# A Householder tridiagonalisation on one Trainium2 core: pivot and divisor as one VectorE operation, placed ahead of a y completion, and part of the next column's seed moved from GpSimd to VectorE

## The reference, cut to what matters

```python
def _L0_gnn_ref(features, A, W1, b1, W2, b2):
    deg = jnp.sum(A, axis=0) + jnp.sum(A, axis=1) - jnp.diagonal(A)
    d_inv_sqrt = jnp.where(deg > 0, jax.lax.rsqrt(deg), 0.0)
    L = jnp.diag(deg) - A
    L_norm = d_inv_sqrt[:, None] * L * d_inv_sqrt[None, :]
    _, U = jnp.linalg.eigh(L_norm)                 # 256 x 256
    agg = jnp.einsum('mn,bnd->bmd', U.T, features)
    h = jax.nn.relu(agg @ W1 + b1)
    return jnp.einsum('nm,bmd->bnd', U, h @ W2 + b2)

h = jnp.maximum(_layernorm(x), 0.0)                # x: 32 x 256 x 128
x = x + _L0_gnn_ref(h, adj, ...)
h = jnp.maximum(_layernorm(x), 0.0)
x = x + _L1_gnn_ref(h, adj, ...)                   # two graph layers, then LSTM windows of 1 to 4 rows
```

## Time and profile before

| | us |
|---|---|
| median of 3 runs | 1600.31 (1600.16 to 1602.43) |
| the profiled execution | 1604.85 |
| its span | 1603.0 |

### The profile page before, as it was taken

How to read it: one execution, slowest core, us unless ns; L and a number is a source line. 1 busy time by engine, 2 the same in 40 slices (tenths; PEclk the granted TensorE clock), 3 DMA queues, 4 the chain that set the end, 5 groups by cost and what they waited for, 6 DMA issues and landing times.

```text
span 1603.0 us, 25379 instructions
## 1 busy us (share of the span) xinstructions
PE 1272.1 (79%) x6001; PEld 1068.2 (67%) x6001; DVE 1246.9 (78%) x6154; ACT 610.2 (38%) x2116; POOL 397.3 (25%) x2138
## 2 busy tenths in 40 slices
PE   6999999999986667777354554365999999999997
PEld 5788888888875555555233333163778789999997
DVE  7999988888788888888899999996772345556555
ACT  1222222222233434322122222251334677878775
POOL 5333333434345555555200000002000010000000
PEclk9999999999999999999977776687999989999999
DMA  7000000000000000000000000000000000001001
GB/s 171 1 1 1 1 1 1 2 1 1 1 1 1 1 1 1 1 2 1 1 0 1 0 1 1 0 1 0 1 1 1 0 1 1 1 1 27 1 27 54
DMA packets 23404, 12.66 MB, mean 8 GB/s; under 512 B 5075, under 2 KB 22230, under 8 KB 23254
## 3 DMA queue, kind: packets, MB, share of 16 engines
q1 hardware_dynamic: 23254, 11.03, 2.8%
HBM read 6.83 MB, written 4.19 MB: 7 GB/s over the span
## 4 chain that ended last, share of the span: by engine, by line
DVE 46%; PE 37%; issue 8%; POOL 7%; ACT 2%; DVEq 1%; POOLq 0%
PE bank L824 8%; PE bank L826 5%; PE bank L833 4%; PE bank L669 4%; DVE A L1046 4%; DVE RC L1134 4%; DVE O L1142 4%; PE bank L672 3%; DVE pa L1130 3%; DVE O L1138 3%; PE pair L824 3%; DVE junk L993 2%; DVE zc L1040 2%; DVE wk L1030 2%; DVE O L1023 2%
## 5 line engine op out<-in xcount | busy, mean ns | idle before, releaser
L672 PEld LDWEIGHTS bank<-O 128*128 128x128 f32 x764 | 201.5, 344 | 0.0
L681 PE MATMUL bank<-O,y 128*128 128x2 f32 x510 | 142.6, 349 | 64.4 <-DVE y L993 59.7
L614 ACT ACTIVATE H<-bank,gate_b 128x128 f32<-128x128 f32 (+2 forms) x468 | 163.3, 434 | 59.0 <-PE bank L826 40.6
L669 PE MATMUL bank<-ident,O 128*128 128x128 f32 x382 | 148.1, 457 | 46.6 <-DVE O L1023 35.6
L477 ACT ACTIVATE ncp<-pc,RC 128x2 f32<-128x2 f32 (+1 forms) x254 | 74.9, 295 | 283.5 <-DVE RC L1014 283.5
L681 PEld LDWEIGHTS bank<-O,y 128*128 128x128 f32 x510 | 129.5, 314 | 75.1 <-issue 72.2
L672 PE MATMUL bank<-O 128*128 128x1 f32 x764 | 162.8, 305 | 0.0
L824 PE MATMUL bank<-O,WlT 128*128 128x128 f32 (+1 forms) x672 | 146.9, 328 | 7.8 <-DVE O L1410 5.6
L689 PE MATMUL pair<-ident,pc 128*128 128x128 f32 x381 | 147.7, 457 | 5.6 <-DVE pc L1012 2.2
L669 PEld LDWEIGHTS bank<-ident,O 128*128 128x128 f32 x382 | 60.2, 198 | 134.4 <-DVE O L1023 134.4
L473 ACT ACTIVATE root<-bank 128x1 f32<-128x1 f32 x255 | 43.7, 171 | 259.8 <-PE bank L672 259.8
(11 more groups left out here) (431 smaller groups left out, 3321.9 us busy)
## 6 DMA issues: line engine op xcount, KB each, us to landing
X<-in_x SPq DMA_DIRECT2D x2, 2048.0 KB, 13.1
out<-X SPq DMA_DIRECT2D x32, 128.0 KB, 1.9
adj_sb<-in_adj SPq DMA_DIRECT2D x1, 256.0 KB, 3.0
W1s<-in_L_gnn_W SPq DMA_DIRECT2D x1, 64.0 KB, 11.1
W2s<-in_L_gnn_W SPq DMA_DIRECT2D x1, 64.0 KB, 4.2
Wg0s<-in_L_gnn_Wg SPq DMA_DIRECT2D x1, 64.0 KB, 3.9
Wg1s<-in_L_gnn_Wg SPq DMA_DIRECT2D x1, 64.0 KB, 3.9
Wl<-in_L_gnn_Wih SPq DMA_DIRECT2D x1, 0.5 KB, 6.7
```

The costliest lines, as they stand in the source:

```text
L614: ins = a(gates[:, q, i, 0:n], gate_at(p, q, i), fn, bias=gate_b[:, p - 1, i:i + 1])
L669: ins = nc.tensor.transpose(xb[:, b * P:(b + 1) * P], R[:, b, k, 0:1].to_broadcast([P, P]), idf)
L672: ins = mm(bank[0][:, 0:1], R[:, b, k, 0:1].to_broadcast([P, P]), R[:, b, k, 0:1], start=(b == bl[0]), stop=(b == 1))
L681: ins = mm(sb_[:, 0:2], y[:, 1:2].to_broadcast([P, P]), R[:, 1, k, :], start=True, stop=(k >= P - 1))
```

## The change

Sigma moves from column 0 to column 1 of bank 0, and column 0 is set to zero once in the start-up. `half` gets a second column, half * x0, written by one more tensor_tensor. One scalar_tensor_tensor then makes the pair (pb, pb * x0 - sigma) as [half, half * x0] * root - [0, sigma]. These two instructions stand ahead of the completion of the upper y; L1004 and L1008 are gone. The wait for xm moves to `cx`. On GpSimd sy, yb and tm are gone; VectorE computes tm = ym * (1 / pb) + tmp by one scalar_tensor_tensor between gqn and the next column.

```diff
@@ GpSimd
-                    pool.wait_ge(S["pb_ready"], k + 1)
-                    g.tensor_tensor(sy[:, bs], tmp[:, bs, c0 + 1], pb.to_broadcast([P, w]), ALU.mult).then_inc(S["sy_ready"], 1)
-                    pool.wait_ge(S["sy_ready"], k + 1)
-                    g.tensor_tensor(yb[:, bs], ym[:, bs], sy[:, bs], ALU.add).then_inc(S["yb_ready"], 1)
-                    pool.wait_ge(S["yb_ready"], k + 1)
                     pool.wait_ge(S["c_ready"], k + 1)
-                    g.tensor_tensor(tm[:, bs], yb[:, bs], RC[:, k, 0:1].to_broadcast([P, w]), ALU.mult).then_inc(S["t_ready"], 1)
@@ ScalarE
-                a(root[:], bank[0][:, 0:1], ACT.Sqrt, scale=4.0).then_inc(S["root_ready"], 1)
+                a(root[:], bank[0][:, 1:2], ACT.Sqrt, scale=4.0).then_inc(S["root_ready"], 1)
@@ TensorE
-                    ins = mm(bank[0][:, 0:1], R[:, b, k, 0:1].to_broadcast([P, P]), R[:, b, k, 0:1], start=(b == bl[0]), stop=(b == 1))
+                    ins = mm(bank[0][:, 1:2], R[:, b, k, 0:1].to_broadcast([P, P]), R[:, b, k, 0:1], start=(b == bl[0]), stop=(b == 1))
@@ VectorE, start-up
+            v.memset(bank[0][:, 0:1], 0.0)
@@ VectorE, the loop
-                sigma = bank[0][:, 0:1]
+                zs = bank[0][:, 0:2]
-                ts(half[:], x0, 0.0, 0.5, ALU.is_lt, ALU.subtract).then_inc(S["half_ready"], 1)
+                ts(half[:, 0:1], x0, 0.0, 0.5, ALU.is_lt, ALU.subtract).then_inc(S["half_ready"], 1)
...
+                dve.wait_ge(S["half_ready"], k + 1)
+                tt(half[:, 1:2], half[:, 0:1], x0, ALU.mult).then_inc(S["hx_ready"], 1)
+                dve.wait_ge(S["hx_ready"], k + 1)
+                dve.wait_ge(S["root_ready"], k + 1)
+                stt(out=NG[:, k, :], in0=half[:], scalar=root[:], in1=zs, op0=ALU.mult, op1=ALU.subtract).then_inc(S["pb_ready"], 1)
                 if b0 == 0:
                     dve.wait_ge(S["y_part"], k + 1)
                     dve.wait_ge(S["y01_ready"], k + 1)
                     stt(out=y[:, 0:1], in0=y01, scalar=below[:, 0, k:k + 1], in1=y[:, 0:1], op0=ALU.mult, op1=ALU.add).then_inc(S["y0_ready"], 1)
-                dve.wait_ge(S["half_ready"], k + 1)
-                dve.wait_ge(S["root_ready"], k + 1)
-                tt(pb, root[:], half[:], ALU.mult).then_inc(S["pb_ready"], 1)
-                if not last:
-                    dve.wait_ge(S["xm_ready"], k + 1)
                 dve.wait_ge(S["pb_ready"], k + 1)
-                stt(out=NG[:, k, 1:2], in0=pb, scalar=x0, in1=sigma, op0=ALU.mult, op1=ALU.subtract).then_inc(S["g1_ready"], 1)
                 if not last:
                     if b0 == 0:
                         dve.wait_ge(S["y0_ready"], k + 1)
                     stt(out=pc[:, bs], in0=A[:, bs, c0], scalar=pb, in1=y[:, bs], op0=ALU.mult, op1=ALU.subtract, reverse1=True).then_inc(S["p_ready"], 1)
-                dve.wait_ge(S["g1_ready"], k + 1)
                 v.reciprocal(RC[:, k, :], NG[:, k, :]).then_inc(S["c_ready"], 1)
                 if last:
                     break
+                dve.wait_ge(S["xm_ready"], k + 1)
                 dve.wait_ge(S["c_ready"], k + 1)
                 tt(cx[:, bs], xm[:, bs], nc_.to_broadcast([P, w]), ALU.mult).then_inc(S["cx_ready"], 1)
                 dve.wait_ge(S["s_ready"], k + 1)
                 stt(out=gqn[:], in0=prn, scalar=s_, in1=y0_, op0=ALU.mult, op1=ALU.subtract, reverse1=True).then_inc(S["gq_ready"], 1)
+                dve.wait_ge(S["ym_ready"], k + 1)
+                stt(out=tm[:, bs], in0=ym[:, bs], scalar=prn, in1=tmp[:, bs, c0 + 1], op0=ALU.mult, op1=ALU.add).then_inc(S["t_ready"], 1)
                 dve.wait_ge(S["t_ready"], k + 1)
                 dve.wait_ge(S["gq_ready"], k + 1)
```

More of the change, by code:

```diff
@@ L108, in gnn_kernel @@
         drow = sb("drow", [P, N]); sq = sb("sq", [P, 2])
-        root = sb("root", [P, 1]); half = sb("half", [P, 1]);
+        root = sb("root", [P, 1]); half = sb("half", [P, 2])
         NG = sb("NG", [P, N, 2]); RC = sb("RC", [P, N, 2]); sh = sb("sh", [P, N])
@@ L115, in gnn_kernel @@
         y = sb("y", [P, 2]); ym = sb("ym", [P, 2]); tm = sb("tm", [P, 2]); pc = sb("pc", [P, 2]); ncp = sb("ncp", [P, 2])
-        xm = sb("xm", [P, 2]); cx = sb("cx", [P, 2]); zc = sb("zc", [P, 2]); sy = sb("sy", [P, 2]); yb = sb("yb", [P, 2]); vt = sb("vt", [P, 2])
+        xm = sb("xm", [P, 2]); cx = sb("cx", [P, 2]); zc = sb("zc", [P, 2]); vt = sb("vt", [P, 2])
         gqn = sb("gqn", [P, 1]); kc = sb("kc", [P, 1]); wk = sb("wk", [P, 1])
@@ L182, in gnn_kernel @@
             lt_rdy adjT_rdy adjT_cp wlt_ps wlt_cp biases
-            x_ready xrow_ready sig_ready root_ready g1_ready y_part y01_ready y0_ready y1_ready half_ready pb_ready p_ready c_ready
-            xm_ready ym_ready vt_ready v_ready kc_ready ncp_ready sy_ready yb_ready t_ready s_ready prow0_ready prow1_ready cx_ready gq_ready w_ready z_ready add0 add1 upd0 upd1 s_hist d0_ready seed_rdy half_upd
+            x_ready xrow_ready sig_ready root_ready y_part y01_ready y0_ready y1_ready half_ready hx_ready pb_ready p_ready c_ready
+            xm_ready ym_ready vt_ready v_ready kc_ready ncp_ready t_ready s_ready prow0_ready prow1_ready cx_ready gq_ready w_ready z_ready add0 add1 upd0 upd1 s_hist d0_ready seed_rdy half_upd
             ln_sum ln_mean ln_var ln_root ln_rstd ln_shift ln_norm
```

## The result

The changed kernel takes 1620.59 us (median of 4 runs, 1620.18 to 1621.14), the kernel before, beside it on the same chip, 1600.24. The ratio is 1.0117, 95% interval 1.0104 to 1.0129: 20 us slower. The profiled execution has a span of 1618.6 us.

The account below looks back on a forecast made before the run. The prediction took a chain of small dependent operations, VectorE busy 86%, to bound the loop. Wide +10, narrow +9, shared operands +1, less 1 for other stalls, made +19 on 1600.3: 1619 us, range 1605 to 1645.

Parts of the forecast that it names:

- part (a): Early wide steps: half*x0 and the pair ahead of y0 cost +0.21 us at k = 36, gone by about k = 72; 11 us.
- part (b): Wide steps, y0 to gqn: gqn waits for TensorE's s_ready, so y0 + 0.90; stretch 0.03 us shorter, not 0.14.
- part (c): Wide steps, tm on VectorE behind gqn: gqn to x 0.38 against 0.33 to 0.36; y0 to x nothing or -1 us.
- part (d): Narrow steps: pair to x 1.11 against 1.12 us, but the pair starts later, +0.14 at k = 165; +9 us.
- part (e): Other engines: earlier GpSimd results gain nothing; VectorE rows running beside GpSimd with two SBUF operands cost 1 us.
- the one of dearer relays: VectorE hand-offs: every dependent start pays 0.10 us, giving 1648; this or a share of it (above 1630), chance 0.20.
- the one of cheaper ones: New VectorE hand-offs as cheap as the cheapest relay row, 0.19 us start to start, giving 1587; chance 0.08.
- The one of the late root: Wide steps: root comes late, y0 queues behind the pair; 0.1 later costs 1 us, inside the range; no separate chance.

## Why the prediction was right

- **The cover in part (a).** Forecast y0 at the read-out + 0.33, a step of 3.70 at k = 36, no loss from about k = 72 on; measured 0.31 and 3.68, and the pair still holds y0 up to about k = 75 (single steps 0.01 to 0.03 longer, too little for the sum of k 64 to 126). Moving y0 forward again took back 7 to 8 us, which stood in the forecast as 11. The mechanism held, the size was a third too large: k 1 to 35 lost 0.15 each and not 0.21, because y0 to x got shorter there. The prediction also took k = 36 for the last step in which VectorE sets y0; in the kernel before y0 stays 0.12 behind the read-out up to about k = 44, so the slope from 36 to 72 was drawn some steps too early.
- **s_ready in part (b).** Forecast gqn 0.90 after y0; measured 0.90 at k = 36 and 0.89 at k = 108, 0.03 to 0.04 behind the end of TensorE's pass. It was the weakest step of the argument, and the swap of cx's waits showed it: cx 0.07 earlier, gqn unmoved.
- **tm in part (c).** Forecast 0.38 from gqn to x, measured 0.39 in wide steps and 0.37 in narrow ones. By itself it costs 8 us, nearly all in narrow steps.
- **Narrow, part (d).** Forecast 1.11 from the pair to x, measured 1.12; forecast +9 us, measured +11. The missing 2 us were in the prediction itself: its own rows give +0.15 at k = 165 (1.43 against 1.28) and +0.03 at k = 223 (1.30 against 1.27) where it wrote 0.14 and 0.02, it counted the last 31 steps as nothing, and it took off 1 us at the end. The 1.12 is also made up of errors that cancel: cx to gqn was 0.10 and not 0.08, RC 0.14 behind pc and not 0.13, against 0.25 and not 0.26 from pair to pc, and 0.24 and not 0.25 from tm to x. The second wait of cx stood in the prediction at 0.07 a step, 9 us; the swap gave 11.
- **GpSimd beside VectorE, part (e).** I put +1 us for operands shared with GpSimd. The x rows of 0.26 are gone instead (k = 108: 3.47 before, 3.43 after, of which 0.04 is this; 37 of 125 wide x rows took 0.25 us or more before, none after), and RC stands 0.17 behind pc in wide steps where I had 0.13, because pc takes 0.25 there instead of 0.22. Both are off the sum: the one is a gain of some 1 us, the other is hidden by s_ready.
- **The whole.** +19 forecast. The loop lost 19.3 us in the profiled execution (754.3 to 773.5), while the untouched rest took 823 us instead of 827 there; the medians differ by 20.4. That the rest differs by 4 us between two executions is not explained by anything I looked at; over the eleven profiled executions the time outside steps 1 to 253 lies between 844 and 849 us, whatever the kernel. The total came closer than its terms: the wide steps lost 2 us less than forecast and the narrow ones 2 us more, and the +1 for shared operands was a gain. That they cancel is luck; the paths and waits behind both halves were right.

Of the rivals, the one of dearer relays is out (hx to pair 0.18, tm to x 0.25, not 0.25 and 0.31), and so is the one of cheaper ones: pair to pc is 0.25, RC to cx 0.26 and tm to x 0.25, none of them 0.19. The one of the late root is out too: at k = 108 the pair starts 0.23 before y0, where 0.14 would do. The rule of the Trainium skill, "VectorE: DVE Perf Modes", section "The DRAIN you can't avoid", that a semaphore between chained operations costs nothing extra, does not carry over to these small operations: the runs show 0.13 between unconnected neighbours (0.07 to 0.08 after a tensor_tensor), 0.18 to 0.25 between dependent ones, and 0.07 more by the order in which two waits are written.

## What to carry to other kernels

Where a step is a relay of small dependent operations, count starts, not busy time: an operation moved ahead of another is free only as long as its neighbour is idle for longer than it takes, so look at that idle time in the first, the middle and the last steps. A fused operation that makes two results makes the consumer of the earlier one wait for both: here that left 0.15 us a step of the 0.26 from pivot to divisor. When a wait moves with an edit, look at what now stands in front of which instruction; the wait for xm, moved to cx, cost more than the fusing saved. And when an instruction has two waits, write first the one that ends last: five such orders were worth 1.5% here, more than the whole change moved.

## What the runs showed of the hardware that I had not expected

- The order of two waits is worth 0.07 us on VectorE, for a semaphore raised by VectorE itself (RC to cx 0.26 and 0.19; pivot to divisor 0.26 and 0.19; gqn to x 0.32 and, with one common semaphore, 0.25), by ScalarE (root's end to the pivot 0.10 and 0.03) and by TensorE (y01's end to y0 0.11 and 0.04). It is about the same where GpSimd waits (y0's end to ym 0.14 and 0.08) and where TensorE does (read-out to gqn 0.83 and 0.77). I had read two sizes of delay out of the trace; that they follow the written order, and how much both kernels would gain by it, the runs showed.
- A dependent operation behind a long pass pays nothing for its wait: zc did not move when its waits were swapped as long as the pass in front had some 55 columns or more. Under shorter passes it stood 0.10 behind wk's end with the bad order; with the good one it followed the pass, down to 0.05 after wk's end under 3 columns.
- A GpSimd row that starts just behind a VectorE row can make that row longer. pc takes 0.24 to 0.25 us where a GpSimd row starts 0.04 to 0.05 after it (some 490 rows of the eleven traces, 157.56 and 157.60 above, sy in the run with tm on GpSimd) and 0.21 to 0.22 otherwise. RC, which starts 0.08 before pc's end in every run, moves with it: 0.17 behind pc instead of 0.14. The run with the orders of the changed kernel put right shows it at the same step k = 36. Its ym comes 0.07 earlier, pc takes 0.22 again and RC follows at 157.70:

```profile
157.53 0.20 POOL L319 TENSOR_TENSOR ym<-y,below 128x2 f32<-128x2 f32 x1 [2.18 <-DVE y L1001]
157.56 0.22 DVE L1006 SCALAR_TENSOR_TENSOR pc<-A,NG,y 128x2 f32<-128x2 f32 x1
```

What the two engines share there, no run isolates.
